# The two large products of a folded low-rank kernel, as 2x2 blocks with seven block products

## The chip, the cores and the metric

The kernel runs on one core of one Trainium2 chip. The metric is the device time of one execution in microseconds (us); of several runs the median is taken. The profile shows one execution on this core.

A core has five engines that run their own instruction streams and meet at semaphores: TensorE (PE), which multiplies matrices and writes to PSUM; VectorE (DVE), ScalarE (ACT) and GpSimd (POOL), which work elementwise; and SyncE (SP), from whose queue all transfers of this kernel are issued.

## What is computed

```
x    [8, 256, 1024] float32, as 4 chunks of 512 tokens (2 items of the batch each)
y  = x + x @ W0.T + 0.5 * (x @ A0[label0]) @ B0.T
z  = y + y @ W1.T + bias + 2.0 * (y @ A1[label1]) @ B1[label1]
```

W0 and W1 are 1024x1024. A0 has 5 tables of 1024x32, B0 is 1024x32. A1 and B1 have 32 tables each of rank 16. Each of the 8 items has its own labels.

Both kernels use that the base parts don't depend on the labels: they form M = (I + W0).T (I + W1).T once (the fold), and then z = x M + low-rank terms. So there are two large products: the fold, 1024x1024x1024, and x M, 2048x1024x1024.

The precision of float32 comes from splitting each operand into hi (rounded to the type float32r, as TensorE takes it) and lo = value - hi, and from three passes: hi*hi, hi*lo, lo*hi.

## The kernel before

A tile has 128 partitions. A matmul takes a stationary operand of 128x128 and a moving one of 128 x up to 512 columns, and adds into one of 8 PSUM banks of 512 columns.

Every operand is split once. ACT copies it to its hi tile, then DVE subtracts hi from it (`split`, L281 to L287); both tiles stay in SBUF as long as they are used. For the diagonal blocks of W0 and W1, POOL adds an identity of 128x128 before that (`add_eye`, L296).

The fold is done in three column parts p of at most 384 columns (`fold_tile`, L132). Part 0 runs with k outside and the 8 output tiles inside, since weights are still arriving; the others with the output tile outside. `keep` (L413) cuts each finished bank into hi (ACT) and lo (DVE). `down_tile` (L143) multiplies B0 into the same parts. A1's tables ride along as 128 columns of part 2.

Then come four chunks c with 8 output tiles o each (`mains`, L188: 8 k by 3 passes, 24 matmuls of 512 columns). `low_a` (L201) has 32 matmuls of 256 columns into bank 7; `low_rows` (L453) takes the rows from it by three ACT copies and one DVE subtraction; `low_f` (L211) needs them, with all of `mains(c, 1)` between. `low_b` (L217) adds two matmuls of 512 columns to each output tile. `finish` (L474) evicts by ACT with the bias and stores the tile; the last tile is done in two halves.

Each engine has one queue in fixed order. For ACT, DVE and POOL it is sorted by an estimated time (`Lane`), for SP likewise (`sp.sort`). PE's order is that of the program (L224 to L238). Waits are on semaphores that count an engine's instructions. A ring of 6 raw tiles holds what arrives by transfer.

Of the kernel before, what the change touches and what calls it, by code (L numbers as in the profile page):

```python
# [12 lines left out]
NC = 4  # L13
T = 512
NK = 8
NO = 8
R = 32
PW = 384
NP = 3
NR = 6  # L20
NZ = 3
WARM = 9
S0, S1 = 16.0 / 32.0, 32.0 / 16.0


class Token:


    def __init__(self):
        self.sem = self.value = None  # L30


class Lane:
# [5 lines left out]
    def put(self, at, waits, emit, token):  # L39
        self.jobs.append((at, len(self.jobs), waits, emit, token))  # L40

# [11 lines left out]

def wait_all(eng, waits, done):
# [6 lines left out]
def bass_fold_and_apply(nc, x, labels, w0, a0, b0, w1, bias, a1, b1, out):  # L61
    ctx = ExitStack()
    with ctx:
        def sb(name, shape, dt):
            return ctx.enter_context(nc.sbuf_tensor(name, shape, dt))
# [32 lines left out]
        def mark(token, s, value):  # L98
            token.sem, token.value = s, value
            return token  # L100


        folded = (pc[3], pc[0], pc[1])

        def v_tile(c, j, k):
            i = 4 * (c % 2) + k // 2
            return w0s[j][:, i, 4 * (k % 2):4 * (k % 2) + 4, :].rearrange("p a c -> p (a c)")

        def columns(half):
            return slice(0, T) if half is None else slice(half * T // 2, (half + 1) * T // 2)  # L110


        prog, now, when = [], 5.0, {}
        bank_free = {}

        def pe(out_ap, lhs, rhs, start, stop, waits=(), name=None, loose=False):
            nonlocal now
            prog.append((out_ap, lhs, rhs, start, stop, tuple(waits), tk(*name) if name else None, loose))
            n = 1
            for s in rhs.shape[1:]:  # L120
                n *= s
            now += n / 2400 + 0.0133
            if name:
                when[name] = now

        def take(bank):
            return [bank_free.pop(bank)] if bank in bank_free else []

        PASSES = ((0, 0), (0, 1), (1, 0))
        uses = 0  # L130

        def fold_tile(p, i, bank, ks):  # L132
            for k in ks:
                for a, b in PASSES:
                    first, end = k == 0 and (a, b) == (0, 0), k == NK - 1 and (a, b) == (1, 0)
                    pe(ps[bank][:, 0:PW], w0s[a][:, i, k, :], pc[p][b][:, k, :], first, end,
                       (take(bank) if first else []) + right_waits(p, k) + [tk("w0", a, k, i // 4)],
                       ("m", p, i) if end else None)

        def right_waits(p, k):  # L140
            return [tk("w1", b, p, k) for b in range(2)] + ([tk("a1", b, h) for b in range(2) for h in range(2)] if p == 2 else [])

        def down_tile(p):  # L143
            nonlocal uses
            bank = uses % 8
            uses += 1
            for k in range(NK):
                for a, b in PASSES:
                    first, end = k == 0 and (a, b) == (0, 0), k == NK - 1 and (a, b) == (1, 0)
                    pe(ps[bank][:, 0:PW], b0s[a][:, k, :], pc[p][b][:, k, :], first, end,  # L150
                       (take(bank) if first else []) + right_waits(p, k) + [tk("b0", a)],
                       ("d", p) if end else None)
            bank_of["d", p] = bank
            bank_free[bank] = tk("dl", p)

        bank_of = {}
        for i in range(NK):
            bank_of["m", 0, i] = uses % 8
            uses += 1
        need = {}  # L160
        for k in range(NK - 1):
            need[k] = now
            for a, b in PASSES:
                for i in range(NK):
                    pe(ps[bank_of["m", 0, i]][:, 0:PW], w0s[a][:, i, k, :], pc[0][b][:, k, :],
                       k == 0 and (a, b) == (0, 0), False, [tk("w1", b, 0, k), tk("w0", a, k, i // 4)])
        need[NK - 1] = now
        for i in range(NK):
            fold_tile(0, i, bank_of["m", 0, i], [NK - 1])
            bank_free[bank_of["m", 0, i]] = tk("ml", 0, i)  # L170
        down_tile(0)
        for p in (1, 2):
            if p == 2:
                down_tile(1)
                down_tile(2)
            for i in range(NK):
                bank = bank_of["m", p, i] = uses % 8
                uses += 1
                fold_tile(p, i, bank, range(NK))
                bank_free[bank] = tk("ml", p, i)  # L180

        tiles = [(c, o) for c in range(NC) for o in range(NO)]
        start_of, uses = {}, 0

        def v_waits(c, j, k):
            return [tk("v", j, c, k)]

        def mains(c, o, half=None):  # L188
            nonlocal uses
            bank = bank_of["z", c, o, half] = uses % 7  # L190
            uses += 1
            p, off = o // 3, 128 * (o % 3)
            start_of.setdefault(c, now)
            for k in range(NK):
                for a, b in PASSES:
                    first = k == 0 and (a, b) == (0, 0)
                    pe(ps[bank][:, columns(half)], folded[p][a][:, k, off:off + 128], v_tile(c, b, k)[:, columns(half)],
                       first, False, (take(bank) if first else []) + [tk("mh" if a == 0 else "ml", p, k)] + v_waits(c, b, k))
            bank_free[bank] = tk("ze", c, o, half)

        def low_a(c):  # L201
            for k in range(NK):
                for j in range(2):
                    for b in range(2):
                        first, end = (k, j, b) == (0, 0, 0), (k, j, b) == (NK - 1, 1, 1)
                        cols = columns(b)
                        pe(pl[:, cols], astk[:, b, k, :], v_tile(c, j, k)[:, cols], first, False,
                           (take(7) + [tk("ah", c), tk("al", c), tk("ac", c)] if first else []) + v_waits(c, j, k),
                           ("la", c) if end else None, True)

        def low_f(c):  # L211
            for b in range(2):
                pe(pl[:, columns(b)], fstk[:, b, :], pstk[0][:, columns(b)], False, b == 1,
                   [tk("fc", c), tk("p0", c), tk("p0l", c)], ("lf", c) if b == 1 else None, True)
            bank_free[7] = tk("p1l", c)

        def low_b(c, o, half=None):  # L217
            bank = bank_of["z", c, o, half]
            pe(ps[bank][:, columns(half)], dstk[:, 128 * o:128 * (o + 1)], pstk[0][:, columns(half)], False, False,
               [tk("p0", c), tk("p0l", c), tk("dl", o // 3)])  # L220
            pe(ps[bank][:, columns(half)], bstk[c % 2][:, 128 * o:128 * (o + 1)], pstk[1][:, columns(half)], False, True,
               [tk("p1", c), tk("p1l", c), tk("bl", c, o // 4)], ("z", c, o, half))

        for c in range(NC):  # L224
            mains(c, 0)
            low_a(c)
            mains(c, 1)
            low_f(c)
            mains(c, 2)
            for o in range(3):  # L230
                low_b(c, o)
# [13 lines left out]
        def load(at, parts, freed, kb, name, before=None):  # L245
# [7 lines left out]
            def emit(eng, done):  # L253
                wait_all(eng, wait, done)
                if before:
                    before(eng)
# [322 lines left out]
```

How the kernel before makes its waits and increments, by code:

```python
    def run(self, eng):  # L47
        done = {}
        for _, _, waits, emit, _ in self.jobs:
            wait_all(eng, waits, done)
            emit(eng).then_inc(self.sem, 1)
# [2 lines left out]
def wait_all(eng, waits, done):  # L54
    for t in waits:
        if done.get(t.sem, 0) < t.value:
            done[t.sem] = t.value
            eng.wait_ge(t.sem, t.value)
# [194 lines left out]
            def emit(eng, done):  # L253
                wait_all(eng, wait, done)
                if before:
                    before(eng)
                for dst, src in parts(raw[n]):
                    eng.dma_start(dst, src).then_inc(s_raw[n], 16)
# [17 lines left out]
            def __call__(self, eng):  # L276
                eng.wait_ge(s_lab, 16)
                for i in self.numbers:
                    value(eng, i, self.top)
# [205 lines left out]
            def emit(eng, done):  # L485
                wait_all(eng, [tk("ze", c, o, half)], done)
                eng.dma_start(out[c, o, :, cols], zt[s][:, cols]).then_inc(s_out[s], 16)
# [19 lines left out]
            @block.sync  # L507
            def _(eng):
                done = {}
                for n, (_, _, emit) in enumerate(sp):
                    if n == 3:
                        eng.dma_start(label_t[:, :], labels).then_inc(s_lab, 16)
                    if n == 30:
                        eng.dma_start(bias_t[:, :], bias).then_inc(s_bias, 16)
                    emit(eng, done)
                for s in range(NZ):
                    eng.wait_ge(s_out[s], n_out[s])
```

## Time and profile before

| what | us |
|---|---|
| median of 3 runs (328.65 to 329.17) | 328.95 |
| the profiled execution | 329.24 |
| its span, from first to last instruction | 327.1 |
| PE busy in it | 323.1 |
| ACT busy | 94.5 |
| DVE busy | 76.6 |
| POOL busy | 16.3 |

The profiled execution is 2.14 us longer than its span; that part lies ahead of the first and behind the last instruction that the profile shows. Busy time of PE is the union of its matmuls, which overlap each other: one takes 390 ns from start to end while the next starts earlier. How dense the stream is must therefore be read from start to start. In the list of groups, "busy, mean ns" are followed by idle time of the engine ahead of the group and what ended it.

### The profile page before, as it was taken

The numbers are of one execution on the slowest core, as the hardware profiler recorded it, in microseconds if no ns is written. First come the engines' busy times: TensorE is split into PE (matmuls) and PEld (weight loads), VectorE is DVE, ScalarE is ACT, GpSimd is POOL, SyncE is SP. The second block draws the span as 40 slices with busy tenths as digits, with TensorE's granted clock in tenths as the row PEclk, the third lists the DMA queues.
The fourth block names the chain that finished last, engine by engine and source line by source line (L and its number), as shares of the span: only waits on it lengthen the run. The fifth ranks groups of instructions, "written<-read, shape, count | busy, mean of one in ns | idle before, by whom it ended". The sixth has DMA issues, their size and how long they took to land.

```text
span 327.1 us, 4085 instructions
## 1 busy us (share of the span) xinstructions
PE 323.1 (99%) x1651; PEld 289.9 (89%) x1651; DVE 76.6 (23%) x125; ACT 94.5 (29%) x172; POOL 16.3 (5%) x45
## 2 busy tenths in 40 slices
PE   8999999999999999999999999999999999999996
PEld 6999999999999999888889888888888888988886
DVE  4868282111264110222020141020033010000000
ACT  4656171111143112343030542120262220222011
POOL 2332010000000011000000100000100000000000
PEclk9999999999999999999999999999999999999999
DMA  6885254100144000051325042325015231003101
GB/s 212 257 274 174 82 147 124 38 0 0 34 151 140 0 0 2 0 192 64 80 83 192 2 126 98 98 96 192 2 50 174 80 101 46 0 2 119 42 34 64
DMA packets 19781, 29.25 MB, mean 89 GB/s; under 512 B 3122, under 2 KB 8626, under 8 KB 19762
## 3 DMA queue, kind: packets, MB, share of 16 engines
q1 hardware_dynamic: 19762, 28.98, 27.8%
q8 instruction: 13, 0.21, 0.3%
q14 instruction: 6, 0.05, 0.0%
HBM read 20.58 MB, written 8.39 MB: 89 GB/s over the span
## 4 chain that ended last, share of the span: by engine, by line
PE 99%; ACT 0%; DVE 0%; issue 0%
PE ps L541 97%; PE ps L537 1%; ACT zt L480 0%; DVE fstk L407 0%
## 5 line engine op out<-in xcount | busy, mean ns | idle before, releaser
L480 ACT ACTIVATE zt<-ps,bias_t 128x512 f32<-128x512 f32 (+1 forms) x33 | 21.8, 676 | 100.8 <-PE ps L541 100.8
L286 DVE TENSOR_TENSOR w0l<-raw,w0h 128x512 fp32r<-128x512 f32 x48 | 32.9, 707 | 57.8 <-ACT w0h L285 57.5
L541 PE MATMUL ps<-w0l,pc3h 128*128 128x512 f32 x96 | 37.5, 390 | 0.0
L541 PE MATMUL ps<-w0h,pc3h 128*128 128x512 f32 x96 | 37.4, 390 | 0.0
L541 PE MATMUL ps<-w0h,pc3l 128*128 128x512 f32 x96 | 37.4, 389 | 0.0
L541 PE MATMUL ps<-w0h,pc0h 128*128 128x512 f32 x96 | 37.3, 389 | 0.0
L541 PE MATMUL ps<-w0l,pc0h 128*128 128x512 f32 x96 | 37.3, 389 | 0.0
L541 PE MATMUL ps<-w0h,pc0l 128*128 128x512 f32 x96 | 37.3, 389 | 0.0
L285 ACT ACTIVATE w0h<-raw 128x512 fp32r<-128x512 f32 x48 | 28.4, 626 | 6.4 <-POOL raw L297 4.6
L541 PE MATMUL ps<-w0l,pc1h 128*128 128x512 f32 (+1 forms) x72 | 26.3, 365 | 0.0
L541 PE MATMUL ps<-w0h,pc1l 128*128 128x512 f32 (+1 forms) x72 | 26.3, 365 | 0.0
L541 PE MATMUL ps<-w0h,pc1h 128*128 128x512 f32 (+1 forms) x72 | 26.3, 365 | 0.0
L541 PEld LDWEIGHTS ps<-w0h,pc3l 128*128 128x128 f32 x96 | 18.0, 188 | 3.8
L541 PE MATMUL ps<-pc1h,w0h 128*128 128x384 f32 x64 | 21.4, 334 | 0.0
L541 PE MATMUL ps<-pc1l,w0h 128*128 128x384 f32 x64 | 21.4, 334 | 0.0
L541 PE MATMUL ps<-pc1h,w0l 128*128 128x384 f32 x64 | 21.4, 334 | 0.0
L541 PE MATMUL ps<-pc2h,w0h 128*128 128x384 f32 x64 | 21.4, 334 | 0.0
L541 PE MATMUL ps<-pc2l,w0h 128*128 128x384 f32 x64 | 21.4, 334 | 0.0
L541 PE MATMUL ps<-pc2h,w0l 128*128 128x384 f32 x64 | 21.4, 334 | 0.0
L541 PEld LDWEIGHTS ps<-w0h,pc0h 128*128 128x128 f32 x96 | 18.0, 188 | 3.8
L541 PEld LDWEIGHTS ps<-w0l,pc0h 128*128 128x128 f32 x96 | 18.0, 188 | 3.7
L541 PEld LDWEIGHTS ps<-w0h,pc0l 128*128 128x128 f32 x96 | 18.0, 188 | 3.7
(84 smaller groups left out, 468.6 us busy)
## 6 DMA issues: line engine op xcount, KB each, us to landing
raw<-in_x SPq DMA_DIRECT2D x32, 256.0 KB, 3.5
out_z<-zt SPq DMA_DIRECT2D x31, 256.0 KB, 2.0
raw<-in_w SPq DMA_DIRECT2D x16, 256.0 KB, 3.3
raw<-in_w SPq DMA_DIRECT2D x16, 192.0 KB, 2.8
raw<-in_b SPq DMA_DIRECT2D x64, 32.0 KB, 1.7
raw<-in_w SPq DMA_DIRECT2D x8, 128.0 KB, 2.3
raw<-in_a SPq DMA_DIRECT2D x8, 128.0 KB, 2.0
raw<-in_a SPq DMA_DIRECT2D x8, 64.0 KB, 1.9
```

The lines of the kernel that those rows point to most:

```text
L285: act.put(at, src_ready + list(extra), lambda e: e.activation(hi, slot_ap, ACT.Copy, scale=scale), tk(*h))
L286: dve.put(at + 0.7, [tk(*h)], lambda e: e.tensor_tensor(lo, slot_ap, hi.bitcast(F32), ALU.subtract), freed)
L480: act.put(at, [tk("z", c, o, half), tk("bias")] + spare, lambda e: e.activation(zt[s][:, cols], bank[:, cols], ACT.Identity, bias=bias_t[: ...
L537: ins = eng.matmul(pl[:, :], zeros, zeros.unsqueeze(1).to_broadcast([128, 4, 128]), start=True, stop=True)
L541: ins = eng.matmul(out_ap, lhs, rhs, start=first, stop=end, skip_group_check=loose)
```

## The change

Each product is done in 2x2 blocks by the scheme of Strassen in Winograd's form. A stage multiplies a 1024x1024 left operand by a 1024x1024 right one; there are three: the fold (stage 0), chunks 0 and 1 (stage 1), chunks 2 and 3 (stage 2). With left blocks A and right blocks B of 512x512, `ORDER` lists seven block products:

```
S1 = A21+A22   S2 = S1-A11   S4 = A12-S2   S3 = A22-S2
T1 = B12-B11   T2 = B22-T1   T3 = T2-B11   T4 = B21-T2
ORDER = (("A11","B11"), ("A12","B21"), ("S1","T1"), ("S4","B22"), ("S2","T2"), ("S3","T3"), ("A22","T4"))
```

- The left operand of stages 1 and 2 is the folded matrix; S1 to S4 of it are formed once in stage 1 and used again in stage 2. The T sums are formed in each stage.
- The sums (`combine`) are elementwise on tiles of 128x512. In stage 0, S1, S4, T2, T3 and S3 run on POOL, S2, T1 and T4 on DVE. In stages 1 and 2 all run on POOL: 20 + 32 + 16 sums there.
- Operands are kept unsplit, and split for each product into rings: A tiles into two halves of a double buffer (`split_a`, which waits for the product before the last), B tiles into a ring of six (`split_b`, which waits for `Bk`, the step k in the last tile of a product, that frees a slot). In the product a tile is one of four row blocks, `tile(n, i)`, 4 k by 3 passes: 12 matmuls of 512 columns.
- Three chains of partial sums stay in PSUM over several products ("a", "c", "b"), and after each product `kept` takes the running sum out: by ACT after products 0 and 1 of a stage, by DVE with an addition after the others.
- The identity is added by DVE for A11 and B11, by POOL for A22 and B22. The weights load in block order into tiles that are not a ring; x is loaded into the same tiles later, each load waiting for the splits and sums of the block that it replaces.
- The low-rank parts are laid anew. In stage 0: `down` and `across` (80 matmuls of 512 columns in all), a small product `fd` (16 of 128 columns), two transposes by identity (`ct_turn`, 16 of 128 columns). In stages 1 and 2 `low_a` and `low_f` have the same matmuls as before, but between `low_a` and `low_f` there is one tile of 12 matmuls. `low_b` again has two matmuls of 512 columns for each of 32 output tiles.
- The last tile is one of 512 columns; its eviction and store are in two halves, on DVE.
- The lanes are still sorted by estimated times, which now follow from the tokens that a job waits for, but hold no time for an engine's queue. A sum on POOL is estimated at 2.2 us, one on DVE at 0.75.

The core of the diff:

```diff
-NR = 6
-NZ = 3
+NB = 6
+NRAW = 3
+ORDER = (("A11", "B11"), ("A12", "B21"), ("S1", "T1"), ("S4", "B22"), ("S2", "T2"), ("S3", "T3"), ("A22", "T4"))
...
+        def split(waits, spare, src, hi, lo, h, l, scale=1.0):
+            act.put(waits + spare, lambda e: e.activation(hi, src, ACT.Copy, scale=scale), h, 0.75)
+            dve.put([h], lambda e: e.tensor_tensor(lo, src, hi.bitcast(F32), ALU.subtract), l, 0.8)
+        def split_a(n, k):
+            stage, name = n // 7, ORDER[n % 7][0]
+            src = where[stage, name][:, k, :].rearrange("p (o c) -> p o c", o=4)
+            spare = [tk("P", n - 2, 3)] if n >= 2 else []
...
+            split([tk("f", stage, name, k)], spare, src, hi, lo, tk("A", 0, n, k), tk("A", 1, n, k))
+        def split_b(n, k):
...
+            m = 4 * n + k - NB
+            spare = [tk("Bk", m // 4, m % 4)] if m >= 0 else []
...
+        def combine(lane, took, stage, name, k, one, other, op, place, spare):
+            where[stage, name] = place
+            ins = [where[stage, b][:, k, :] for b in (one, other)]
+            lane.put([tk("f", stage, b, k) for b in (one, other)] + spare,
+                     lambda e: e.tensor_tensor(place[:, k, :], ins[0], ins[1], op), tk("f", stage, name, k), took)
...
+        def step(n, i, k, end=None):
+            bank = chain_banks(n // 7, CHAIN[n % 7])[i]
+            for a, b in PASSES:
...
+                pe(ps[bank][:, :], ar[n % 2][a][:, i, k, :], b_tile(n, k, b), opens, False, waits, name)
+        def tile(n, i):
+            for k in range(4):
+                step(n, i, k, ("P", n, i) if k == 3 else None)
...
+        def kept(n, i, done, half=None):
...
+            elif p == 3:
+                used = [tk("B", 1, n - 1, i), tk("f", stage, "T2", i)]
+                dve.put([done] + used, lambda e: e.tensor_tensor(w, z, s1, ALU.add), token, 0.75)
...
+        ON_POOL, ON_DVE = (pool, 2.2), (dve, 0.75)
...
+            tile(n + 1, 0)
+            for k in range(4, 8):
+                low_a(c0, cc[3], k, *x_ring(n + 1)(k - 4))
+            low_rows(c0, "p0", tk("la", c0), 0, cc[3], 0)
+            tile(n + 1, 1)
+            low_f(c0, cc[3])
...
+            for i in range(4):
+                tile(n + 6, i)
+                low_b(stage, 0, 1, i, ab[i], False, ("z", stage, "21", i))
+                for half in ((0, 1) if last and i == 3 else (None,)):
+                    kept(n + 6, i, tk("z", stage, "21", i), half)
```

## Rows read from the trace of the kernel before

**Rows 1.** Summary page: busy time, granted clock in 40 slices, chain by engine.
```profile
PE 323.1 (99%) x1651; PEld 289.9 (89%) x1651; DVE 76.6 (23%) x125; ACT 94.5 (29%) x172; POOL 16.3 (5%) x45
...
PEclk9999999999999999999999999999999999999999
...
PE 99%; ACT 0%; DVE 0%; issue 0%
```

**Rows 2.** Chain that ended last: start us, length us, what.
```profile
1.26 4.21 PE ps L537 x9
...
5.54 318.92 PE ps L541 x1642
...
324.49 0.47 ACT zt L480
```

**Rows 3.** Timeline of PE: start us, length us, engine, line, instruction, count.
```profile
10.68 1.55 PE L541 MATMUL ps<-pc0h,w0h 128*128 128x384 f32 x8
...
12.07 1.55 PE L541 MATMUL ps<-pc0l,w0h 128*128 128x384 f32 x8
...
127.92 0.40 PE L541 MATMUL ps<-w0l,astk 128*128 128x256 f32 x2
...
128.16 0.40 PE L541 MATMUL ps<-w0h,pc3h 128*128 128x512 f32 x1
...
205.78 0.39 PE L541 MATMUL ps<-w0h,pc0h 128*128 128x512 f32 x1
...
218.70 0.39 PE L541 MATMUL ps<-w0h,pc1l 128*128 128x512 f32 x1
```

**Rows 4.** Groups by line and shape: busy us, mean ns, idle before and releaser.
```profile
L286 DVE TENSOR_TENSOR w0l<-raw,w0h 128x512 fp32r<-128x512 f32 x48 | 32.9, 707 | 57.8 <-ACT w0h L285 57.5
L285 ACT ACTIVATE w0h<-raw 128x512 fp32r<-128x512 f32 x48 | 28.4, 626 | 6.4 <-POOL raw L297 4.6 <-DMA raw<-in_w 1.6
...
L297 POOL TENSOR_TENSOR raw<-raw,eye 128x128 f32<-128x128 f32 x16 | 10.5, 661 | 35.5 <-DMA raw<-in_w 35.5
...
L444 POOL CAST astk<-pc1h 128x128 fp32r<-128x128 f32 x8 | 2.3, 293 | 169.8 <-PE ps L541 97.3 <-DVE pc1l L418 72.5
...
L450 POOL CAST fstk<-dstk 128x16 fp32r<-128x16 f32 x8 | 1.3, 197 | 14.1 <-PE ps L541 14.1
```

**Rows 5.** Stretches at the start (last: clock, transfer share, GB/s); page's GB/s by slice.
```profile
6.00:10.00 4.00, 4.00 (x21) 4.00 (x21) 2.50 (x5) 2.22 (x5) 2.06 (x4) 1.00 0.92 319
10.00:15.00 5.00, 5.00 (x30) 5.00 (x30) 4.40 (x7) 3.69 (x7) 1.37 (x2) 1.00 0.90 264
...
GB/s 212 257 274 174 82 147 124 38 0 0 34 151 140 0 0 2 0 192 64 80 83 192 2 126 98 98 96 192 2 50 174 80 101 46 0 2 119 42 34 64
```

**Rows 6.** Timeline of POOL and DVE around 9 us.
```profile
8.87 1.02 POOL L297 TENSOR_TENSOR raw<-raw,eye 128x128 f32<-128x128 f32 x1 [0.69 <-DMA raw<-in_w]
8.87 0.69 DVE L286 TENSOR_TENSOR w0l<-raw,w0h 128x512 fp32r<-128x512 f32 x1 [0.23 <-ACT w0h L285]
...
9.48 0.95 DVE L286 TENSOR_TENSOR w0l<-raw,w0h 128x512 fp32r<-128x512 f32 x1
9.84 0.91 POOL L297 TENSOR_TENSOR raw<-raw,eye 128x128 f32<-128x128 f32 x1
```

**Rows 7.** The line L297 by itself: duration min/median/max in ns.
```profile
L297 POOL TENSOR_TENSOR raw<-raw,eye x16: 453/622/1017, 3.6 to 47.3; 128x128 f32<-128x128 f32 x16
```

**Rows 8.** Timeline of ACT and DVE behind low_a and behind low_f, chunk 0.
```profile
128.36 0.59 ACT L459 ACTIVATE pstk<-ps 32x512 fp32r<-32x512 f32 x1 [8.82 <-PE ps L541]
...
129.58 0.59 ACT L461 ACTIVATE pstk<-ps 32x512 fp32r<-32x512 f32 x1
...
130.21 0.68 DVE L462 TENSOR_TENSOR pstk<-ps,pstk 32x512 fp32r<-32x512 f32 x1 [10.08 <-ACT pstk L461]
...
135.29 0.59 ACT L461 ACTIVATE pstk<-ps 32x512 fp32r<-32x512 f32 x1
...
137.29 0.69 DVE L462 TENSOR_TENSOR pstk<-ps,pstk 32x512 fp32r<-32x512 f32 x1
```

More of the change, by code:

```diff
@@ new lines, in bass_blocks, with down @@
+        for k in range(4):
+            load_w("A11", k)
+            load_w("B11", k)
+        load_small()
+        for k in range(4):
+            load_w("A12", k)
+            load_w("B21", k)
+        for k in range(4):
+            load_w("A21", k)
+            load_w("A22", k)
+            load_w("B12", k)
+        for k in range(4):
+            load_w("B22", k)
+        X, Y = range(0, 4), range(4, 8)
+        def down(bank, n, h, start, end):
+            for k in range(4):
+                for j in range(2):
+                    first = k == 0 and j == 0
+                    last = k == 3 and j == 1
+                    name = end if last else ("Bk", n, k) if n == 0 and j == 1 else None
+                    pe(ps[bank][:, :], b0s[:, 4 * h + k, :, :].rearrange("p q r -> p (q r)"), b_tile(n, k, j), first and start, False,
+                       (take(bank) if first and start else []) + [tk("b0l"), tk("B", j, n, k)], name)
@@ L133, in fold_tile, with across @@
+        def across(bank, h, moving, moving_waits, start, end, ks=range(4)):
             for k in ks:
                 for a, b in PASSES:
[L135 to L141, printed above, removed]
@@ L188, in mains @@
[L188 to L199, printed above, removed]
@@ L201, in low_a @@
[L201 to L222, printed above, removed]
@@ new lines, in four_done, with ct_split @@
+        def four_done(*name):
+            return [tk("four", q, *name) for q in range(4)]
+        def ct_split(bank, done, half):
+            spare = [tk("tr", 0)] if half else []
+            act.put([done] + spare, lambda e: e.activation(ct[0][:, :], ps[bank][:, :], ACT.Copy), tk("ct_h", half), 0.7)
+            dve.put([tk("ct_h", half)], lambda e: e.tensor_tensor(ct[1][:, :], ps[bank][:, :], ct[0][:, :].bitcast(F32), ALU.subtract), tk("ct_l", half), 0.75)
+            bank_free[bank] = [tk("ct_l", half)]
@@ new lines, in bass_blocks @@
+        rows_sum(X[0], tk("dn", 3), slice(0, 512), 0, dtmp[2][:, :], ("d2",), four_done("d", 0) + [tk("sum", "d", 0)])
+        bank_free[X[0]] = [tk("sum", "d2")]
+        dve.put([tk("sum", "d2")], lambda e: e.tensor_tensor(dtmp[2][:, :], dtmp[2][:, :], dtmp[1][:, :], ALU.add), tk("sum", "d", 1), 0.7)
+        four_rows(dtmp[2][:, :], dstk[:, 512:1024], tk("sum", "d", 1), ("d", 1))
+        for i in range(1, 4):
+            tile(3, i)
+            kept(3, i, tk("P", 3, i))
+        took_by = {"B11": "B12", "B21": "B22", "B12": "B11", "B22": "B21"}
```

856 lines of the change are left out of this document (544 added, 312 removed).

## The prediction, made before the changed kernel was run

> **What bounds the kernel now.** I read the summary of busy time first: TensorE (PE) is busy 99% of the span, VectorE (DVE) 23%, ScalarE (ACT) 29%, GpSimd (POOL) 5%, and the granted clock is full in every slice, which is the 2.4 GHz level [rows 1]. Busy matmuls can still be slow ones, so the chain that ended last comes next: 318.92 of 327.1 us are one unbroken run of 1642 matmuls, ahead of it 9 warm-up matmuls, behind it one ACT eviction and a store [rows 2]. Last, whether that run is dense, from start to start: 512 columns 12.92 us for 57 matmuls (205.78 to 218.70), 0.2267 us each; 384 columns 1.39 us for 8, 0.173; 256 columns 0.24 for 2, 0.120 [rows 3]. So 0.0533 us go with 128 columns, plus 0.0133 us per matmul. The program has 648 matmuls of 384 columns, 806 of 512 (744 in the main tiles, 62 in low_b) and 188 of 256: 112.3 + 182.7 + 22.6 = 317.6 us of the 318.9. Stalls are 1.3 us, all at the start. Only fewer or shorter matmuls help; other engines have room, and how much of it the change uses up is the question.
>
> **The matmuls.** After the change each of three stages (the fold of the weights, then two pairs of token chunks) has 7 block products of 4 tiles x 4 k x 3 passes = 48 matmuls: 3 x 7 x 48 = 1008 of 512 columns. The low-rank work of stage 0 (down, across, side_across) has 32 + 48 = 80 of 512; its transposes and the small product fd 32 of 128. low_b has 64 of 512; low_a and low_f have 136 of 256. Sum: 1152 x 0.2267 = 261.2, 136 x 0.120 = 16.3, and 32 of 128 columns, for which no row stands: 0.067 us each by the line through the three widths, 0.120 if they go no faster than those of 256; near the middle 3.0 us. That is 280.5 us for 317.6: **37.1 us less**. The eighth product saved per stage would be 3 x 10.9 = 32.6 us; the rest is 384-column tiles becoming 512 (fewer fixed parts), and other low-rank sums.
>
> **The start.** Before, the stream starts at 5.54 [rows 2]. Afterwards A11 and B11 tiles come first, with the same ACT and DVE steps (0.626 and 0.707 us [rows 4]) behind two additions on DVE: unchanged within 1 us, counted 0. Product 0 needs 512 KB for each 2.72 us of matmuls, 193 GB/s; the transfers ran at 264 to 319 GB/s [rows 5]. The tiles up to B12 are 8.0 MB: at 264 GB/s from 3 us they have landed at 33.3, and the identity, S1 on POOL, hi and lo (0.46 + 1.26 + 0.63 + 0.71) follow by 36.4. S1 is wanted at 5.5 + 1.3 + products 0 and 1 (21.8) + 40 matmuls of 512 and 16 of 128 = 39, its last k 2 us later. Cover 4.6 us: nothing.
>
> **The end.** The last tile is one of 512 columns, evicted as two halves by DVE, one behind the other, where an ACT eviction of 256 took 0.47 us [rows 2]: +0.4 us (0 to 1).
>
> **The splits.** Every operand tile is split as it comes up, again for each product: hi on ACT, lo on DVE. Per product that is 8 hi, 8 lo and 4 evictions that add to a kept block (mostly DVE). Queued DVE operations of 512 follow each other after 0.61 us (8.87 to 9.48) [rows 6]. A bare product lasts 48 x 0.2267 = 10.9 us; ACT needs some 8 x 0.63 = 5.0, DVE 12 x 0.61 = 7.3. So both fit, DVE at 67%; over the program DVE has 168 lo, 12 side, 61 + 8 block additions, 12 sums and some 50 smaller ones, near 200 us of 290. The B ring holds six tiles: tiles k=2 and 3 of the next product can be overwritten only once the last tile of the running one has passed k=0 and k=1. From there: 0.3 to ACT's start, 0.63, 0.71, so lo is ready some 2.4 us after the last tile began, and it is wanted at 2.72 + 1.36 = 4.1. Cover 1.7 us: nothing, if DVE is free. If it isn't, PE stands.
>
> **The sums on POOL.** 68 additions of 128x512 move there (20 + 32 + 16 in the three stages). No row has one. An undisturbed 128x128 addition takes 0.453 us, copies of 128 and 16 columns 0.293 and 0.197 [rows 4, 7]. The copies put 0.183 us as the fixed part, so the addition goes at 2.11 ns a column and one of 512 takes 1.26 us; bounds are 1.17 (four copies) and 2.64 (four additions at their mean of 0.661). I take 1.26: 86 us over the program. The GPSIMD Engine Reference of the Trainium skill (section 3.1) has 2.6 cycles per element for this two-input addition, 1.11 us for 512 by its clock ahead of the fixed cost; no run here shows that length yet.
>
> The 0.661 us is the warning. A POOL addition that starts with DVE's at 8.87 takes 1.02 us, and the DVE operation behind that one 0.95 us instead of 0.69; then POOL's next takes 0.91 [rows 6]. These lengths add up if each waits for the other in turn: DVE 0.61, POOL 0.4, DVE 0.6, POOL 0.4. The Trainium skill, SBUF — State Buffer, section "Who interferes with whom", states this as a rule: a DVE instruction with two SBUF inputs contends with a GpSimd instruction that reads SBUF, and an exclusive port lets one pass whole. By that rule, and the trace agrees, the sums are not free although POOL has 95% of its time left; without it the 3 us below would be 0. Priced from rows: a long addition holds DVE's lo operations up by up to 512 x 2.11 = 1.08 us. Evictions, whose one input is PSUM, I take as not held. Where POOL has work without a break, a product costs DVE 8 x (0.61 + 1.08) = 13.5 us, the evictions in POOL's shadow, against PE's 10.9: 2.6 us short per product. POOL has such a stretch where stage 1 begins: T1, S1, S2, S4 of stage 1, then S3 and the first half of the T sums, some 28 of 68, come due within products 5 to 8. Products 5 and 6 are bare; 7 and 8 carry 1.9 to 4 us of low-rank matmuls that lend cover. Two products at 2.6, at half to two thirds of that since the sums arrive in pieces: **3 us** (0 to 4 products at 2.6 = 10). Stage 2 has 16 sums and hardly such a stretch.
>
> **The low rows.** low_f needs the rows p0, which ACT and DVE cut from low_a's bank. In the trace that is ACT at 128.36 (0.32 behind the start of low_a's last matmul, the second of the pair at 127.92), three copies, DVE from 130.21 to 130.89: 2.85 us behind 128.04 [rows 8]. Before, 24 matmuls (5.4 us) lay between; now one tile of 12, 2.72 us. Even with idle queues each of the four low_f comes 0.15 us short. In the second chain of this trace DVE came to the rows at 137.29 although ACT had them at 135.88 [rows 8]: 1.4 us. So 0.15 to 1.5, with a POOL addition ahead 2.6 us each; 0.9 x 4 = **3.6 us** (0.6 to 10). Behind the waiting low_f stand all matmuls of that product.
>
> **The rest of stage 0.** side_across waits for two splits whose slots come free only 2.7 us before, in the stretch where POOL does 20 sums; ct_turn waits for ct_split; sums (T4) on DVE wait for POOL with splits queued behind. I take **2 us** (0 to 6). SP's queue takes x loads that wait for lo of B tiles and for T sums, with stores behind them, and kept waits for stores; these have about a product of slack, so 0. On POOL the small copies into fstk stand behind sums and are due a product later: 0. A gain apart from the matmuls is excluded, since before has no other stall.
>
> **Sum.** Span 327.1 - 37.1 + 0.4 + 3 + 3.6 + 2 = 299.0. The profiled run took 329.24, 2.14 beyond its span; that gives 301.1, and as the median of the runs is 0.29 below the profiled one, **300.8 us**.
>
> **Rivals.**
> A. All of it hides: low_f at 0.15 each, no contention on PE's path. 327.1 - 37.1 + 0.4 + 0.6 = 291.0 span, 292.9. For it: the totals (DVE 67% of a bare product). Against: rows 8 leave low_f no cover. Up to 296: 15%.
> B. DVE and POOL serialise in more stretches (stage 0 with 20 sums, all of stage 1 with 32): ten of the products short by 1.5 to 2.6, or queues in fixed order blocked by a late POOL sum. With the top ends of low_f that is 15 to 30 us above A: 306 to 322. For it: 200 us of DVE and 68 x 1.08 = 73 us of held port are 273 of 290. Against: only 8 of 12 DVE operations per product are of the kind held, and sums come in bursts. 24%.
> C. Slower than before: the same mechanism in the extreme, each POOL sum keeping PE waiting for its 1.08 us. A leaves 328.95 - 292.9 = 36.1 us, so it decides from 36.1 / 1.08 = 34 of the 68 on; all 68 with A's base give 366. For it: in-order queues. Against: stage 0's sums fall in products with 2.6 to 8 us of other matmuls. 3%.
> D. The matmul stream comes out longer than counted, because operands in F32 tiles or 512-column weights read other than before: excluded but for 128-column matmuls at 0.8 us. That transfers starve the fold: at 212 GB/s, the rate of the first slice, B12 is there at 40.7, its products' operands at 43.8 instead of 41, and PE loses 3 us; that lies within the range.
>
> **Numbers.** My forecast, 296 to 306: 57%. A, 15%; B, 24%; C, 3%; same, 1%. Two in ten may be left out: 293 to 313. A measurement of this kernel tells about 0.2% from no change. Faster 0.96, same 0.01, slower 0.03.
>
> **What would show it.** PE's spacing at 0.2267 in 48-matmul products and about 280 us if gaps are left out; gaps of 0.2 to 1.5 us ahead of each low_f with DVE as releaser; POOL additions of 1.26 us alone and near 1.9 in company, DVE's lo above 0.69 on average while evictions stay at 0.69; gaps at the head of products 6 and 7. Wrong would be: gaps in all products (B), waits of ACT for POOL with splits queued behind (order), or a clock below full after a long gap.

## The result, and the profile after

| what | us |
|---|---|
| before, median of 4 runs beside it | 329.06 |
| after, median of 4 runs (331.42 to 334.18) | 332.75 |
| ratio | 1.0113, 95% [1.0068, 1.0159] |
| the profiled execution of after | 331.42 |
| its span | 329.7 |

The change makes the kernel 1.1% slower. Forecast were 300.8, range 293 to 313. The profiled execution of after is the fastest of its four, 1.3 us below the median; all accounts by product below are of profiled executions, and so don't add up to differences of medians exactly. The page of after: busy times, POOL and granted clock in 40 slices, the chain by engine.

```profile
PE 299.1 (91%) x1329; PEld 242.4 (74%) x1329; DVE 241.7 (73%) x315; ACT 152.1 (46%) x271; POOL 118.3 (36%) x89
...
PE   7999925999999698997999899999957999999995
...
DVE  3599999989689599994648498997445648387631
...
POOL 0008999930031899960081004552100054000000
PEclk9999985899999969999999999999989999999999
...
PE 51%; DVE 29%; POOL 7%; ACT 5%; issue 3%; SPq 3%; DMA 2%; DVEq 0%; ACTq 0%; POOLq 0%
```

Against [rows 1]: 1651 matmuls have become 1329. PE is down from 99% to 91%, though half-speed matmuls count as busy there. The chain that ended last (of work and waits, followed back from the last instruction) runs on other engines than PE for 49% of the span. PE has three holes: slices 6 and 7 (of 8.2 us each, counted from 1), where POOL and DVE both read 9; slice 14, with POOL at 8; and 30 and 31, where POOL reads 0, so that it must have another cause. The clock falls with each or one slice later (5 in slice 7, 6 in 15).

Measured from start to start as in [rows 3], the 1320 matmuls behind the 9 of the warm-up split up as follows. At the spacings of before, and with the estimate of 0.067 us for 128 columns, they would take 279.6 us (317.6 before). All that goes beyond these spacings, called excess here, is 40.1 us. Products are numbered through the three stages, 0 to 20, seven to a stage:

| product | excess, us | what |
|---|---|---|
| 0 | 2.0 | first tiles come one at a time |
| low-rank of stage 0, 1, 3 | 1.2 | 128-column matmuls 0.11 apart, not 0.067 |
| 2 | 15.1 | stands for S1's last tile (6.9, 2.4, two of about 1), half clock behind it |
| 6 | 7.0 | hi of ring slot 2 (`br2h`) 1.5, its lo (`br2l`) 2.4, half clock |
| 7 | 2.0 | `br0l`, `br1l` |
| 8, 10 | 2.8, 2.0 | low_f 1.9 each, one lo 0.7 |
| 15 | 7.3 | `br2h` 3.5, half clock, low_f 1.9 |
| 4, 5, 9, 11, 12, 14, 16, 18 to 20 | 0 to 0.04 | |
| 13, 17 | 0.7 together | |

A bare product (4, 5, 12, 19) takes 10.88 us, which is 48 x 0.2267. So 38.0 us of matmuls went away, and 40.1 came back as stalls, with 0.8 more at the start and 0.8 at the end: 327.1 - 38.0 + 40.1 - 1.3 (the stalls of before) + 0.8 + 0.8 = 329.5, against a span of 329.7; the rest is rounding of the spacings.

PE's waits in after, by releaser: us in total, times, longest.

```profile
PE ps L865 <- ACT ar0h L191: 6.6, 1, 6.6
PE ps L865 <- DVE pstk L650: 5.2, 3, 1.7
PE ps L865 <- ACT br2h L191: 4.7, 2, 3.3
PE ps L865 <- DVE ar0l L192: 2.9, 2, 2.0
PE ps L865 <- DVE br2l L192: 2.2, 1, 2.2
```

**POOL and DVE in each other's way.** Groups by line of after (busy us, mean ns, idle before), against 707 ns for `lo` in [rows 4].

```profile
L226 POOL TENSOR_TENSOR w_B<-w_B 128x512 f32<-128x512 f32 x20 | 32.5, 1650 | 12.9 <-DVE br2l L192 6.9 <-DVE br0l L192 4.6 <-DVE br1l L192 1.3
L226 POOL TENSOR_TENSOR w_A<-w_A 128x512 f32<-128x512 f32 x12 | 21.2, 1790 | 0.8 <-DVE w_A L226 0.7
L192 DVE TENSOR_TENSOR ar1l<-m,ar1h 128x512 fp32r<-128x512 f32 x16 | 19.7, 1273 | 0.0
...
L419 DVE TENSOR_TENSOR m<-ps,m 128x512 f32<-128x512 f32 x12 | 8.0, 683 | 0.3 <-PE ps L865 0.2
```

And the timeline: a sum while DVE is idle, three `lo` and two sums in company (start us, length us).

```profile
108.41 1.29 POOL L226 TENSOR_TENSOR m<-m 128x512 f32<-128x512 f32 x1 [5.29 <-DVE m L419]
...
122.31 5.17 DVE L192 TENSOR_TENSOR ar1l<-m,ar1h 128x512 fp32r<-128x512 f32 x3
...
123.49 1.74 POOL L226 TENSOR_TENSOR w_A<-m 128x512 f32<-128x512 f32 x1
125.19 1.74 POOL L226 TENSOR_TENSOR m<-m 128x512 f32<-128x512 f32 x1
```

Alone a sum takes 1.29 us. In company both engines deliver one operation each 1.70 us: 123.49 to 125.19 for POOL, 5.17 / 3 for DVE. That is 0.61 + 1.08 = 1.69, with 1.08 the column part of a sum as the prediction priced it. Both engines have work nearly without a break through 25 to 69 us (POOL busy 42.2 of 44, DVE 43.1), and POOL does through 108 to 145 (36.6 of 37, DVE 33.4). The two don't always take turns: the sum at 42.87 lasted 2.64 us, beside two DVE operations of two SBUF inputs that ran at their full speed (43.11 and 43.71, 0.67 each). The one at 217.67 lasted 4.02 us, while DVE went through five `lo` from 217.45 on at 0.60 to 0.61 each. There it was POOL alone that was held; what decides between the two cases is open. The eviction, whose other input is PSUM, stays at 683 ns.

**Product 2.** What PE waits for at 50.95, followed back.

```profile
42.87 5.99 POOL L226 TENSOR_TENSOR w_A<-w_A 128x512 f32<-128x512 f32 x3
48.82 0.89 POOL L277 TENSOR_TENSOR w_B<-w_B,eye 128x128 f32<-128x128 f32 x1
...
49.74 0.63 ACT L191 ACTIVATE br0h<-w_B 128x512 fp32r<-128x512 f32 x1 [2.80 <-POOL w_B L277]
50.28 0.61 ACT L191 ACTIVATE ar0h<-w_A 128x512 fp32r<-128x512 f32 x1
...
50.95 0.80 PE L865 MATMUL ps<-br5h,ar0h 128*128 128x512 f32 x1 [6.61 <-ACT ar0h L191]
```

The three sums are, by the order of POOL's queue, S4 (k=2), S1 (k=3) and S3 (k=2). Product 2 needs S1 only; S4 is due a product later and S3 three. `ar0h`, the hi of that S1 tile, could have gone once its sum was done, at 47.2, but stands in ACT's queue behind `br0h`, which belongs to the next product and waits for an identity on POOL: 3.1 of the 6.6 us. So POOL's slowness reaches PE through two fixed orders.

**The clock.** PE's timeline behind that gap, and two windows (us; busy of PE, PEld, DVE, ACT, POOL; granted clock; transfer share; GB/s).

```profile
54.80 0.63 PE L865 MATMUL ps<-ar0h,a1h 128*128 128x512 f32 x1
55.22 0.63 PE L865 MATMUL ps<-ar0l,a1h 128*128 128x512 f32 x1
55.65 0.63 PE L865 MATMUL ps<-ar0h,a1l 128*128 128x512 f32 x1
```

```profile
50.00:60.00 10.00, 7.02 (x16) 5.05 (x17) 10.00 (x8) 5.43 (x11) 10.00 (x8) 0.50 0.14 38
...
240.00:250.00 10.00, 6.66 (x30) 5.17 (x29) 5.68 (x9) 6.42 (x13) 0.00 (x0) 0.83 0.06 15
```

The granted clock falls while PE stands (0.60 over 46 to 48 us) and is 0.50, the 1.2 GHz level, until 60 us; matmuls start each 0.427 us, not 0.227. The same is seen around the gaps that end at 115.7 and 244.6. 26 spacings of this kind cost 5.2 us, near 7 with those beside the gaps. A gap doesn't always bring this: the three of 1.9 us ahead of low_f leave the clock at 1.00. Nor does its length decide: the pairs of runs below have nearly the same gap with and without the fall.

### The profile page after: what moved, and what is told of

Same layout as the page of the kernel before. It is cut to its first block, busy times and chain, and to the rows that moved or that the text cites. A ratio compares the mean times of both kernels' runs of the same rounds, so it can differ in the third digit from the quotient of the medians.

```text
span 329.7 us, 3892 instructions
## 1 busy us (share of the span) xinstructions
PE 299.1 (91%) x1329; PEld 242.4 (74%) x1329; DVE 241.7 (73%) x315; ACT 152.1 (46%) x271; POOL 118.3 (36%) x89
## 4 chain that ended last, share of the span: by engine, by line
PE 51%; DVE 29%; POOL 7%; ACT 5%; issue 3%; SPq 3%; DMA 2%; DVEq 0%; ACTq 0%; POOLq 0%
PE ps L865 51%; DVE ar1l L192 5%; DVE ar0l L192 4%; POOL w_A L226 4%; SPq L141 3%; DVE br3l L192 2%; POOL w_B L226 2%; DVE br5l L192 2%; DVE astk L192 2%; DVE m L419 1%; DVE br4l L192 1%; DVE br2l L192 1%; DVE br0l L192 1%; DMA raw<-in_b 1%; DVE w_B L226 1%
## 5 line engine op out<-in xcount | busy, mean ns | idle before, releaser
L226 POOL TENSOR_TENSOR w_B<-w_B 128x512 f32<-128x512 f32 x20 | 32.5, 1650 | 12.9 <-DVE br2l L192 6.9
L226 POOL TENSOR_TENSOR keep_w<-w_B 128x512 f32<-128x512 f32 x8 | 10.8, 1355 | 48.5 <-DMA w_B<-in_x 33.4
L192 DVE TENSOR_TENSOR ar0l<-w_A,ar0h 128x512 fp32r<-128x512 f32 x28 | 20.8, 771 | 2.8 <-ACT ar0h L191 2.8
L226 POOL TENSOR_TENSOR w_A<-w_A 128x512 f32<-128x512 f32 x12 | 21.2, 1790 | 0.8 <-DVE w_A L226 0.7
L192 DVE TENSOR_TENSOR ar1l<-m,ar1h 128x512 fp32r<-128x512 f32 x16 | 19.7, 1273 | 0.0
L192 DVE TENSOR_TENSOR ar1l<-w_A,ar1h 128x512 fp32r<-128x512 f32 x24 | 19.1, 828 | 0.0
L191 ACT ACTIVATE ar0h<-w_A 128x512 fp32r<-128x512 f32 x28 | 16.5, 623 | 5.3 <-DVE w_A L277 4.6
L865 PE MATMUL ps<-br2l,ar0h 128*128 128x512 f32 x32 | 13.1, 409 | 2.3 <-DVE br2l L192 2.2
L192 DVE TENSOR_TENSOR ar0l<-m,ar0h 128x512 fp32r<-128x512 f32 x16 | 14.7, 956 | 0.1
L191 ACT ACTIVATE ar1h<-w_A 128x512 fp32r<-128x512 f32 x24 | 14.0, 625 | 0.2
L226 POOL TENSOR_TENSOR w_A<-m,w_A 128x512 f32<-128x512 f32 x8 | 13.7, 1737 | 0.0
L650 DVE TENSOR_TENSOR pstk<-ps,pstk 32x512 fp32r<-32x512 f32 x8 | 5.5, 683 | 11.1 <-ACT pstk L649 11.1
```

The costliest lines, as they stand in the source:

```text
L191: act.put(waits + spare, lambda e: e.activation(hi, src, ACT.Copy, scale=scale), h, 0.75)
L192: dve.put([h], lambda e: e.tensor_tensor(lo, src, hi.bitcast(F32), ALU.subtract), l, 0.8)
L226: lambda e: e.tensor_tensor(place[:, k, :], ins[0], ins[1], op), tk("f", stage, name, k), took)
L650: dve.put([tk(stage, c)], lambda e: e.tensor_tensor(dst[R:2 * R, :], g[0], dst[0:R, :].bitcast(F32), ALU.subtract), tk(stage + "l", c), 0.75)
L865: ins = eng.matmul(out_ap, lhs, rhs, start=first, stop=end, skip_group_check=True)
```

## The experiments

All change the kernel after. Those that share a chip share the runs of before (329.06, 328.82 and 328.97 in the three groups). "Less than after" compares medians with 332.75; ratios are to before.

### 1. The 68 sums, off POOL or shortened

**sums_dve**: the engine alone.

```diff
-        ON_POOL, ON_DVE = (pool, 2.2), (dve, 0.75)
+        ON_POOL, ON_DVE = (dve, 0.75), (dve, 0.75)
```

> Edit: all 68 sums of the changed kernel that ran on POOL run on DVE; nothing else. Changed kernel: 332.8 us. Theory P (a POOL sum holds the shared SBUF port 1.08 us against DVE's splits, rival B of the prediction): a sum on DVE costs its 0.61 us instead of 1.08 us of waiting, the pair of lo and sum goes from 1.70 to 1.21 us, so the gaps of products 2, 6, 7 and 8 (15.1 + 7.0 + 2.0 + 0.9 us of excess, half clock in them included) shrink by about half: 318 to 324 us, lo at 0.69 mean everywhere. Theory D (DVE simply has too much work): 41 us more of DVE work make it worse: over 336 us. Theory Q (the gaps come from jobs that wait in fixed queue order for late loads): no change but from the new order, 330 to 336 us.

Measured 321.84, ratio 0.977 [0.9753, 0.9788]: 10.9 us less than after. This lies in the range of theory P. DVE does 68 more operations and is busy 234.8 us, where it was 241.7: what POOL held it up is more than what the 68 sums cost on DVE itself. But excess stays: product 2 8.7, product 6 7.9.

```profile
109.50 0.69 DVE L226 TENSOR_TENSOR m<-m 128x512 f32<-128x512 f32 x1
110.11 0.68 DVE L192 TENSOR_TENSOR br2l<-w_B,br2h 128x512 fp32r<-128x512 f32 x1
...
110.85 0.79 PE L865 MATMUL ps<-br2l,ar0h 128*128 128x512 f32 x1 [4.64 <-DVE br2l L192]
```

In this timeline PE waits 4.6 us for a `lo` that stands behind sums for the stage to come (11 from 101.1 us on, each holding the queue for 0.60 us), none of which this product or the next needs. So a second mechanism is likely, the order in which an in-order queue is filled; sections 2 and 3 take it by itself.

**sums_short**: on POOL as in after, but 60 of the 68 do only 16 of their 512 columns (T1 stays whole). The kernel leaves out the rest of the block sums; every wait and every order stays.

```diff
+            n = 16 if lane is pool and name != "T1" else 512
```

> Edit: the 60 sums on POOL other than T1 do only their first 16 of 512 columns, so the values of the block sums are not computed; every wait and every order stays. Theory P: the port is free, lo at 0.69, the gaps of products 2, 6 (the later part), 7 and 8 go, with the half clock behind them: 308 to 316 us. Theory Q: POOL was never what the gaps waited for; products 6 and 15 keep their gaps of 1.5 and 3.5 us ahead of the B split and product 2 keeps its gap because the A21 and A22 tiles come late: 324 to 332 us. What is left in this run besides the three gaps of 1.9 us ahead of low_f is what the sums have nothing to do with.

310.41, ratio 0.9432 [0.9413, 0.9451]: 22.3 us less than after, with the same queues and the same transfers. Product 2's excess falls from 15.1 to 1.3, that of product 6 from 7.0 to 4.2, that of product 7 from 2.0 to 0 and that of product 15, in which POOL has no sums, from 7.3 to 5.9; product 10 keeps its 2.0, and product 8 the 1.9 us of low_f. This doesn't say whether POOL was too slow or in the way.

**sums_filler**: as sums_short, and ahead of each short sum POOL fills 1024 columns of a scratch tile, which keeps it busy and reads nothing.

```diff
+                pool.put(waits + [last], lambda e: e.memset(fill, 1.0), mine, 0.0)
```

> Edit: as in the run with short sums (60 POOL sums do 16 of 512 columns, block sums not computed), but ahead of each POOL first fills 1024 columns of a scratch tile with a constant, about a microsecond in which it only writes. So POOL is as slow as in the changed kernel but reads no SBUF in that time. Short sums took 310.4 us, the changed kernel 332.8. Theory P1 (DVE is held because both read SBUF through one port): DVE's lo stays at 0.69 and the time is 310 to 315 us, about all of the 22 us is the port. Theory P2 (the products wait for the sums themselves, which come one behind the other from a slow engine): 322 to 331 us though lo stays at 0.69. If lo rises above 0.8, writes hold DVE too and the run tells nothing apart.

308.07, ratio 0.9372 [0.935, 0.9394]. Groups by line:

```profile
L232 POOL MEMSET scratch<- 128x1024 f32 x60 | 57.2, 953 | 32.2 <-DVE side0l L193 24.3 <-DVE m L427 7.4
...
L234 POOL TENSOR_TENSOR w_B<-w_B 128x16 f32<-128x16 f32 x20 | 5.8, 292 | 1.6
L193 DVE TENSOR_TENSOR ar0l<-m,ar0h 128x512 fp32r<-128x512 f32 x16 | 10.3, 687 | 0.1
```

Fill and short sum are 0.95 + 0.29 = 1.24 us, near the length of an undisturbed full sum (1.29). POOL is thus about as slow as it is by itself, and PE doesn't mind: 24.7 us less than after. It is DVE held up, and POOL held up by DVE, that cost 22 to 25 us, the part of the order that only shows under it included. That this run is even 2.3 us faster than sums_short, below the expected 310 to 315, is the clock: both have nearly the same gaps (1.3 and 1.2 us in product 6, 1.63 and 1.67 in product 15), but behind them sums_short has 11 half-speed spacings and this run none that aren't of its start. The Trainium skill, SBUF — State Buffer, section "Who interferes with whom", says that a DVE operation with two SBUF inputs contends with a GpSimd one that reads SBUF and not with one that only writes it; the trace agrees, with 687 ns beside the fills.

### 2. ACT's copies of B1, and the low rows

**b1_late**: in ACT's queue the copies of B1 for (1,1) and chunk 3 come later.

```diff
+                hold = now + 20.0 if (c, h) == (1, 1) else now + 2.0 if c == 3 else 0.0
...
-                act.put([tk("raw", "b1", c, h)] + spare, lambda e, hi=hi, slot=slot: e.activation(hi, raw[slot][:, :], ACT.Copy, scale=S1), tk("bh", c, h), 0.75)
+                act.put([tk("raw", "b1", c, h)] + spare, lambda e, hi=hi, slot=slot: e.activation(hi, raw[slot][:, :], ACT.Copy, scale=S1), tk("bh", c, h), 0.75, hold)
```

In after, ACT stands at such a copy, and the split for PE behind it:

```profile
238.64 0.63 ACT L626 ACTIVATE bstk<-raw 128x512 fp32r<-128x512 f32 x1 [7.57 <-DMA raw<-in_b]
242.45 0.63 ACT L626 ACTIVATE bstk<-raw 128x512 fp32r<-128x512 f32 x1 [3.18 <-DMA raw<-in_b]
242.99 1.07 ACT L396 ACTIVATE keep_s<-ps 128x512 f32<-128x512 f32 x2
243.94 0.63 ACT L191 ACTIVATE br2h<-w_B 128x512 fp32r<-128x512 f32 x1
```

and SP's queue for those sixteen transfers of 32 KB:

```profile
233.67 7.37 SPq L141 DMA_DIRECT2D raw<-in_b  x16
```

> Edit: ACT's copies of the B1 rows of chunk 1 (second half) and of chunk 3 get a later place in ACT's queue (20 us and 2 us behind the time at which they are put), so that splits and evictions no longer stand behind copies whose 8 small transfers have not landed. Theory Q: product 15 loses its excess of 5.2 us but for the low_f gap (3.5 us gap, 0.8 us half clock, 0.9 us rest), product 6 loses the gap of 1.5 us and part of the 2.45 us behind it: 324 to 328 us. Theory P alone: product 15 still, since no POOL sum runs there, but product 6 keeps 5 us or more of its 7.0: 327 to 329 us. Where the copies were not the cause: 332 to 333 us.

325.56, ratio 0.9893 [0.9877, 0.991]: 7.2 us less, in the range of theory Q. Product 15 goes from 7.3 to 2.0, the low_f alone. That is 5.3 of the 7.2 us. Product 6 goes from 7.0 to 0, but 7 and 8 go from 2.0 and 2.8 to 5.1 and 6.0; the three together from 11.8 to 11.1. There the wait was passed on, to waits for DVE (`br0l` 2.4, `pstk` 3.3). That DVE was behind through POOL in any case is my reading of it; this run alone doesn't show it.

**rows_early**: the DVE step of `low_rows` waits for the second ACT copy, not the third, and so also sorts ahead of the `astk` splits.

```diff
-            dve.put([tk(stage, c)], lambda e: e.tensor_tensor(
+            dve.put([tk(stage + "b", c)], lambda e: e.tensor_tensor(
...
-            bank_free[bank] = [tk("p1l", c)]
+            bank_free[bank] = [tk("p1", c), tk("p1l", c)]
```

In after, DVE and PE:

```profile
252.31 0.69 DVE L192 TENSOR_TENSOR astk<-raw,astk 128x512 fp32r<-128x512 f32 x1 [2.57 <-ACT astk L191]
252.92 0.49 DVE L192 TENSOR_TENSOR astk<-ctile,astk 128x128 fp32r<-128x128 f32 x2
253.44 0.68 DVE L650 TENSOR_TENSOR pstk<-ps,pstk 32x512 fp32r<-32x512 f32 x1
...
254.27 0.47 PE L865 MATMUL ps<-pstk,fstk 128*128 128x256 f32 x2 [1.75 <-DVE pstk L650]
```

ACT had the rows at 251.63 (its third copy runs from 251.04 for 0.59). DVE comes at 253.44, behind three splits for the next chunk, which wait for ACT.

> Edit: DVE's subtraction for the low rows waits for ACT's second copy instead of the third (the third reads other partitions), and by that comes ahead of the astk splits in DVE's queue. In the changed kernel PE stands 1.9 us ahead of low_f three times: ACT copies end 4.0 us into the wait, then a copy into astk and three DVE subtractions (1.1 us), then the rows. Theory R (the gap is the queue order ACT third copy, astk, rows): each of the three gaps goes to 0 to 0.3 us, the time falls by 5 us: 327 to 329 us. Rival (low_f has no cover at all, 2.85 us of chain against one tile of 2.72 us, and what is gained on DVE is lost to ACT's third copy): each gap falls to 0.5 or more, 329 to 331 us.

326.14, ratio 0.9906 [0.9889, 0.9923]: 6.6 us less, a little more than the expected 5; between the profiled executions it is 5.0. The three gaps of 1.9 are gone, product 10 is at 0.04.

### 3. The order of the sums

**lazy_pool**: the sums stay on POOL; each gets a due time, so that it sorts in near the product that needs it.

```diff
+            first, pace = DUE[min(stage, 1), name]
...
-                     lambda e: e.tensor_tensor(place[:, k, :], ins[0], ins[1], op), tk("f", stage, name, k), took)
+                     lambda e: e.tensor_tensor(place[:, k, :], ins[0], ins[1], op), tk("f", stage, name, k), took, now + first + pace * k)
```

> Edit: the sums stay on POOL and whole; each gets a due time so that its place in the queues is shortly ahead of the product that needs it, spread at one per 2.2 to 2.5 us, where in the changed kernel a sum is queued as soon as its operands exist. Nothing else. Theory of bursts (rival B's loss comes from stretches in which POOL has work without a break; spread, each sum holds DVE once and DVE's 67% leave room for it): products 6, 7 and 8 lose their contention part (about 8 of 9.8 us; the wait for the late rows of B1 in product 6 stays) and product 2 most of its 15 us, as S4, T2, T3 move behind its splits: 312 to 320 us. Rival (each hold reaches PE anyway): 326 us or more.

323.71, ratio 0.986 [0.9831, 0.989]: 9.0 us less. Both theories missed: it lies above 312 to 320 and below 326. Product 2 falls from 15.1 to 6.6, but product 6 keeps 6.7, and 12 and 17 now have 1.4 and 3.0: the sums are spread, and so is their contention.

**lazy_dve**: all four: sums on DVE, due times, b1_late, rows_early.

> Edit: all sums on DVE with the same due times as in the spread POOL version, and the late place of the B1 copies and the early low rows of the other two runs. The single edits gave 321.8 (all on DVE), 325.6 (B1) and 326.1 us (rows) from 332.8. In the run with all sums on DVE the gaps that were left (product 2: 3.8 + 1.0 us, product 6: 4.9 us, half clock behind them) lay where DVE did a row of sums that were not yet due ahead of a split that was. Theory (work 280.5 us of matmuls, 6.3 start, 2.7 to 4 of the end, start loss 3 us): 296 to 302 us. If DVE were simply full (235 us busy of some 295): 306 us or more, with gaps spread over all products.

**298.65** (298.51 to 299.17), ratio 0.9091 [0.9075, 0.9106]: 34.1 us less than after, 9.1% below before. The four steps alone gave 10.9 + 9.0 + 7.2 + 6.6 = 33.7. Page and PE's waits:

```profile
PE 288.1 (97%) x1329; PEld 238.2 (80%) x1329; DVE 233.9 (79%) x383; ACT 152.4 (51%) x271; POOL 9.1 (3%) x21
...
PE 82%; DVE 12%; ACT 2%; issue 1%; DMA 1%; DVEq 0%
```

```profile
PE ps L870 <- DVE br4l L192: 1.8, 1, 1.8
PE ps L866 <- DVE fstk L177: 1.3, 1, 1.3
PE ps L870 <- DVE pstk L655: 0.8, 2, 0.4
```

Excess is 7.4 us: 1.9 in product 0, 2.1 in product 5, 0.7 each in 10 and 17, 1.2 from 128-column matmuls, the rest small. The clock is 0.998: even the gap of 2.0 us in product 5 leaves it alone. That the four add up so well is no proof that they are independent: due times alone are worth 9.0 with the sums on POOL, and 12.8 in the next pair.

**three** (lazy_dve without due times) and **lazy_pool_all** (lazy_dve with the sums back on POOL) take one step out each.

> Edit: the 298.7 us version without due times: sums on DVE as soon as their operands exist, late B1 copies, early low rows. It prices the order alone. In the run with only the sums on DVE (321.8) product 2 had 8.7 us of excess and product 6 had 7.9, of which some 1 to 2 in product 6 by the B1 rows; the B1 and rows edits take 12 to 14 us elsewhere. Theory (a sum that is not due ahead of a split that is): 307 to 313 us, excess in products 2 and 6. Rival (order of the sums doesn't matter on DVE): under 302 us.

> Edit: the 298.7 us version with the sums put back on POOL; due times, late B1 copies and early low rows stay. It prices the engine of the sums alone where the queue orders are good. Theory P (the port): 60 to 68 sums hold DVE for up to 1.08 us each, of which a part reaches PE: at the 22 us that the changed kernel gained without them 321 us at most; since three edits took waits of another kind away and the sums are spread, 306 to 314 us, with lo means of 0.8 to 1.0 us and gaps in products 2, 6, 10, 12, 17 as in the spread POOL run. Rival (with good queue orders POOL does no harm): under 302 us.

Both lie in the ranges of their theories. three: 311.44, ratio 0.9464 [0.9435, 0.9492]; due times are worth 12.8 us beside the others. Its excess sits in products 2 (8.7) and 6 (7.3), as in sums_dve. lazy_pool_all: 313.82, ratio 0.9549 [0.9513, 0.9585]; the engine is worth 15.2. One group of it, and the same of lazy_dve:

```profile
L192 DVE TENSOR_TENSOR ar0l<-w_A,ar0h 128x512 fp32r<-128x512 f32 x28 | 28.4, 1043 | 2.8 <-ACT ar0h L191 2.8
```

```profile
L192 DVE TENSOR_TENSOR ar0l<-w_A,ar0h 128x512 fp32r<-128x512 f32 x28 | 18.9, 708 | 3.6 <-ACT ar0h L191 3.5
```

With the same good order, POOL's sums still lengthen these `lo` from 708 to 1043 ns, and PE loses 6.3, 5.6 and 5.3 us in products 2, 7 and 17.

### 4. What is left

**lazy_dve2** (S3, T2 and T3 of stage 0 due 1 to 5 us earlier) and **lazy_dve_eye** (the identity of B11 on POOL, for the start).

> Edit: the 298.7 us version with the due times of S3 and T3 of stage 0 moved 3 to 5 us earlier. In it PE stood 2.0 us in product 5 ahead of the first matmul of B's slot 4: ACT's splits of S3 stood ahead of that B split and waited for DVE's sums. Theory: that gap goes, 296.4 to 297.5 us. If the gap is from DVE's load there (it did 24 operations back to back) and not from the order, it only moves: 298 to 299 us.

> Edit: as the run before it, and the identity for B11 is added by POOL instead of DVE. In the changed kernel the first eight tiles go at 1.59 us each in lockstep (identity on DVE, hi on ACT, lo on DVE, each behind the other in queue order), product 0 lasts 12.8 us instead of 10.9. Theory (the lockstep of DVE's queue order): product 0 loses 2 us, time 1.5 to 2.5 us below the run before it. Rival (the transfers of the first 2 MB are what paces it): no difference beyond 0.5 us.

lazy_dve2: 299.06, ratio 0.9089 [0.9062, 0.9115], where the expectation has the gap only move; it is halved in product 5, and 0.6 appears in product 4. lazy_dve_eye: 300.62, ratio 0.9145 [0.9097, 0.9193]; product 0 has 3.1 us, not 1.9: `br0l` now stands in DVE's queue behind the next A tile, for whose transfer DVE waits 0.9 us, and one gap of 1.4 replaces four of 0.35. The half-speed spacings behind it (7, or 1.4 us) can't be put down to the edit: seven runs that have only the gaps of 0.4 there show 5 to 8 of them too. And 1.6 us more lie in product 5, whose gap of 2.0 us is that of lazy_dve, but with a fall of the clock (window, busy PE, granted clock, transfer share, GB/s; lazy_dve first):

```profile
90.00:92.00 2.00, 2.00 (x10) 1.00 0.82 219
```

```profile
90.00:92.00 2.00, 2.00 (x6) 0.50 0.74 239
```

The one execution of lazy_dve_eye with the clock at 1.0 throughout took 298.90. So neither gains, and the 2 us by which its median is worse are mostly the clock.

## Why the prediction was wrong

**The matmuls: held.** 280.5 us were forecast; the trace has 279.6 by the spacings of [rows 3] and 1.2 more for those of 128 columns. Those take 3.5 us for 32, forecast 3.0. The part of rival D on the matmul stream is out.

**POOL beside DVE: right mechanism, wrong stretch.** The price per pair was forecast as 0.61 + 1.08 = 1.69 us and measured 1.70; 1.26 for a sum alone was 1.27 to 1.29; in company the sums took 1.70 to 1.74, where the signs had "near 1.9"; evictions are not held. The step that failed is "Two products at 2.6, at half to two thirds of that since the sums arrive in pieces: **3 us**". It asked only whether a bare product's DVE work fits into 10.9 us, and waved stage 0 through, since its sums "fall in products with 2.6 to 8 us of other matmuls". But those matmuls lend cover only to work for a later product. S1 is needed by product 2 itself, and its last tile comes behind S4 and S3 in the same queue, on an engine at 1.7 us per operation. The forecast of S1 ready at 36.4 took POOL's queue as free; in fact the operand reached PE at 50.95. Product 2 alone lost 15.1 us where I had 2 us for the rest of stage 0. In the stretch that was priced (products 6 to 8) the size was nearer: sums_short has 5.6 us less there, for a forecast 3. In all, sums_short and sums_filler put the contention at 22 to 25 us (with the clock that it costs) against a forecast 3 to 5.

**The order of the queues: named as part of a rival, without a price.** B and the last lines of the prediction had queues blocked by a late sum, and the text noted that the lanes are sorted by estimates that hold no time for the queue. It should have been drawn up: on each engine, what stands ahead of the operand that PE needs next. 12.8 us hang on that with the sums on DVE (three), 4.2 of them in one wait in product 6; with the sums on POOL, as the prediction had them, it is 9.0 (lazy_pool). The two prices of this and the last paragraph overlap, as the ACT queue in product 2 shows.

**Transfers and small steps at 0: wrong.** The weights were issued later than I had taken (A12 from 14.3 us on), yet the last tile of B12 landed at 33.28, just as forecast (33.3), and sums_filler, with the same issues, has 1.4 us of excess in product 2. But B1's copies wait for their transfers on ACT with splits for PE behind them, 6 to 7 us, and they weren't in the text at all. Each transfer issued there holds SP for 0.46 us (7.37 / 16), so sixteen small ones take 7.4 us.

**The low rows: right mechanism, a size too small.** Forecast 0.9 each, four of them, 3.6 us; measured three at 1.9 and one near free (0.2), 5.7, and 6.6 by removal. That is within the stated 0.6 to 10. The releaser is the one named, and the cause beyond the 0.15 is the order (splits ahead), of the kind that [rows 8] showed with 1.4.

**The start and end: small misses.** 0.8 us to the first matmul and 2.0 in product 0 for a forecast 0: A11 and B11 have their identity added on DVE, whose queue puts it behind the `lo` of the tile before, so tiles come one per 1.59 us (`ar0l` at 4.63, `br0l` at 6.22, `ar0l` at 7.82). The end took 0.8, forecast 0.4.

**The clock: named, not in the sum.** "A clock below full after a long gap" stood among the signs. It is 5 to 7 us, and adds about a third to the 16.7 us of the five longest gaps (6.9, 2.4, 1.5, 2.4, 3.5).

**The chances.** C, slower by a wait of PE for more than 34 sums, was right in sign and wrong in form: not single sums that each reach PE, but several queues in a wrong order, each for some us. I gave it 3% because I priced each cause by itself with the others absent. That lazy_dve comes to 298.65, within the forecast range and 0.7% from 300.8, says that the arithmetic of the matmuls was sound; what I called a forecast was near the time of a well-ordered version. How near is partly luck: 8.6 us of the forecast were for contention, low rows and the rest of stage 0, on which lazy_dve loses about 1.6, while it loses 1.9 in product 0, 2.1 in product 5 and 0.6 at the first matmul, which the sum had at 0.

## What to carry to other kernels

When a change takes work from the engine that bounds and hands another one several times what it had (DVE 23% to 73% busy), don't ask whether totals fit into a stage: list for each in-order queue what stands ahead of the next operand, and price cover only for work that a later product needs. Where two-input sums on POOL would hold up DVE, try them on DVE, even if it is the busier one: here that was worth 10.9 and 15.2 us. And give jobs a due time, not only an earliest one.

## What the runs showed of the hardware

- Where both had work, two-input operations of 128x512 on DVE and POOL mostly alternated at 1.70 us per pair (two of the 68 sums took longer, 2.64 and 4.02), and moving POOL's to DVE made DVE less busy (241.7 to 234.8 us). ACT stays at 0.61 to 0.63 us beside both.
- Beside POOL fills of 128x1024 (953 ns), DVE's `lo` of the group shown stayed at 687 ns.
- DVE operations of 32 partitions by 512 columns with two SBUF inputs are held like full ones: 1.57 us at 112.39, 0.68 at 106.86.
- Around gaps of PE its granted clock can drop to 0.50 for some us, and the gap's length alone doesn't decide: at 2.0 us in product 5 it stayed at 1.00 in lazy_dve and fell in lazy_dve_eye; at 1.63 and 1.67 in product 15 it stayed in sums_filler and fell in sums_short; at 2.9 us ahead of the low_f of product 17 it stayed in lazy_pool. What else decides is open.
- SP's queue issued nothing from 5.5 to 10.3 us, where the program has it read the eight labels that address the next transfers. No wait of PE was seen to come from it: product 1 has 0.1 us of excess.
